# Attention layer with feed-forward on one core: causal weights cleared by GpSimd, normalisation transfers on SP, two head operations on ScalarE

## Chip, core and metric

The kernel runs on one core of one Trainium2 chip. The metric is the device time of one execution in microseconds (us), as a median over runs. Engines are named as in the profile: PE is TensorE, DVE is VectorE, ACT is ScalarE, POOL is GpSimd, SP is SyncE.

## The reference, cut to what matters

```python
# x: (4, 1024, 512), 16 heads of 32
mod = (silu(c) @ wmod).reshape(4, 6, 1, 512)          # sa, ca, ga, sb, cb, gb
h = layernorm(x) * (1 + ca) + sa
q = (layernorm(h, qn_g, qn_b) @ Wq + bq)              # k, v alike, with kvn and Wkv
q, k = rotary(q * scale, h), rotary(k * scale, h)     # turned, times the norm of h
qn, kn = layernorm(q, ln_g, ln_b), layernorm(k, ln_g, ln_b)   # over each head's 32
scores = where(causal, qn @ kn.T / sqrt(32), min)
a = softmax(scores) @ v
x = x + ga * (a @ Wo + bo)
h = layernorm(x) * (1 + cb) + sb
x = x + gb * ((silu(h @ Wg.T) * (h @ Wu.T)) @ Wd.T)
```

Everything is float32. Where precision needs it, products use the two halves (hi and lo) of a number in the type fp32r.

## The kernel before

Four stages run one after the other, each a block with one instruction stream per engine: `qkv_stage`, `attention_stage`, `project_stage`, `ffn_stage`. The streams meet at semaphores only; each engine takes its instructions strictly in the order in which they stand.

**qkv_stage** works through 32 tiles of 128 rows. `stagger` writes each engine's stream: step u runs the functions of a list in the order of the list, each on tile u minus its lag. In step u DVE runs `norm_h` (tile u-3), `norm_x` (u-1), `stat_h` (u-2), `stat_x` (u), `turn` (u-5, the rotary products out of PSUM), `low` (u-3), `means` (u-6), `spread` (u-7). ACT runs `scale_x` (u-1), `high` (u-3), `root_h`, `root_x`, `take_v` (u-5), `square_h` (u-2), `square_heads` (u-6), `factor` (u-7). POOL runs `shift_x` (u-1), `norm_heads` (u-8), `rotate` (u-5), `centre` (u-6). PE runs `turn_h` (u-3, four transposes) and `product` (u-4, 39 matmuls). The head normalisation of q and k goes through three engines: `rotate` on POOL, `means` on DVE (a sum over each head at L397 and its scaling to `hmean` at L399), `centre` on POOL, `square_heads` on ACT, `spread` on DVE (a sum at L404, `ms2h` at L405, `den` at L407, a reciprocal at L409), `factor` on ACT, `norm_heads` on POOL.

**attention_stage** works through 16 groups (a batch entry and four heads). A group has 12 steps k, numbered w = 0 to 11. In a step PE writes two shift matmuls of the step's block into `psB`, then two score items into `psA` (only their maximum over keys is taken, by DVE, `peak`), then two more shift matmuls, in w = 1 and 3 a transposition of q or k for the group ahead (`prepare`), in w = 0 the transposition of the peaks, and then `weigh` of the block shifted one step before: the weights `probT` times v into `psO` and times ones into `psL`. ACT turns each shift result into weights (`exponent`, L950), with two buffers in `psB` and three in `probT`. `BLOCKS` has 12 blocks a group, (half, kb); a block whose key tile touches the diagonal (8 of the 12, numbers 0 to 3 and 8 to 11) gets a mask matmul behind each of its four shift matmuls (L825). Blocks run 14 steps behind the scores: block 0 of a group in w = 2, block 11 in w = 1. The chain `prepare` (PE), `widen` (ACT), `high` (POOL, L753), `low` (DVE, L876) makes the next group's operands; score items and `prepare` take turns in the two halves of `psA`, so each waits for what stood two turns before.

`normalise(n)` on POOL sends the sums of the weights to DRAM, reads them back spread over 128 partitions, waits for DVE's reciprocal, writes them out, reads them back widened, and multiplies `att` with them (L767), all in w = 3 of group n+2:

```python
            def normalise(n):
                pool.wait_ge(s["taken_l"], 2 * n + 2)
                pool.dma_start(scratch["sums"][0], sums[0:P:HD, n % 2]).then_inc(s["sums_out"], 16)
                pool.wait_ge(s["sums_out"], 16 * n + 16)
...
                pool.wait_ge(s["wide_in"], 64 * n + 64)
                pool.wait_ge(s["taken_o"], 2 * n + 2)
                pool.tensor_tensor(att[:, n % 2], att[:, n % 2], sums[:, n % 2], ALU.mult).then_inc(s["scaled"], 1)
```

Of the kernel before, what the change touches and what calls it, by code (L numbers as in the profile page):

```python
# [111 lines left out]
def qkv_stage(nc, args, scratch):  # L112
# [4 lines left out]
    with ExitStack() as ctx:  # L117
# [3 lines left out]
        def sem(name):  # L121
# [28 lines left out]
        ms2h = sb("a_ms2h", [P, 8])  # L150
# [24 lines left out]
                 "rec_ready fac_ready qk_ready").split()  # L175
# [11 lines left out]
        rows1_out, mod_in = sem("rows1_out"), sem("mod_in")  # L187
        late_copied, late_step, late_out = sem("late_copied"), sem("late_step"), sem("late_out")
# [19 lines left out]
        def _(sp):  # L208
# [4 lines left out]
            def load(b, t):  # L213
# [36 lines left out]
            sp.wait_ge(late_step, 4)  # L250
            for m in range(2, 6):
                at, n = late_place(m)
                sp.wait_ge(late_copied, m - 1)
                sp.dma_start(scratch["mod"][:, m, :], late[at, n]).then_inc(late_out, 16)
            for j in range(4):
                sp.wait_ge(stored[j], 32 * NT // 4)
            sp.wait_ge(late_out, 16 * 4)
# [34 lines left out]
        def _(dve):  # L292
# [101 lines left out]
            def means(b, t):  # L394
# [15 lines left out]

            stagger(dve, B, TB, [(norm_h, 3), (norm_x, 1), (stat_h, 2), (stat_x, 0), (turn, 5), (low, 3), (means, 6), (spread, 7)])
# [4 lines left out]
            dve.tensor_scalar(size[two], late[two], -1.0, None, ALU.mult).then_inc(late_step, 1)  # L416
            dve.wait_ge(late_step, 1)
            dve.tensor_tensor(size[two], size[two], late[two], ALU.max).then_inc(late_step, 1)
            dve.wait_ge(late_step, 2)
            dve.tensor_scalar(size[two], size[two], 0.25, None, ALU.max).then_inc(late_step, 1)  # L420
            dve.wait_ge(late_step, 3)
            dve.scalar_tensor_tensor(out=late[two], in0=sign[two], scalar=-1.0, in1=size[two], op0=ALU.add, op1=ALU.mult).then_inc(late_step, 1)

        @block.scalar
        def _(act):
# [152 lines left out]
def attention_stage(nc, args, scratch):  # L578
# [12 lines left out]
    BUFS = 3  # L591

# [38 lines left out]
    with ExitStack() as ctx:  # L631
# [3 lines left out]
        def sem(name):  # L635
# [18 lines left out]
        probT = sb("b_probT", [P, 3, 4, W])  # L654
# [9 lines left out]
                 "peaks_turned peaks_copied peaks_in shifted expd weighed summed taken_o taken_l sums_out few_in inverted few_out "  # L664
# [17 lines left out]
        def _(sp):  # L682
# [36 lines left out]

            load(0)  # L720
# [4 lines left out]
            for k in STEPS:  # L725
# [9 lines left out]
                if w == 10 and 0 <= n - 2 < NG:  # L735
                    store(n - 2)
# [3 lines left out]
        def _(pool):  # L740
# [708 lines left out]
```

## Time and profile before

| | us |
|---|---|
| median of 3 runs | 2458.92 (2458.35 to 2460.32) |
| the profiled execution, its own time | 2456.73 |
| its span in the profile | 2454.6 |
| PE busy | 2279.7 (93%) |
| DVE busy | 1165.7 (47%) |
| ACT busy | 793.3 (32%) |
| POOL busy | 728.3 (30%) |

The busy shares are means over four stages that differ. qkv_stage ends near 392 us of the span, attention_stage runs from about 400 to about 1200, the feed-forward stage from about 1400 to the end. In the page's 40 slices DVE shows 9 tenths in the first stage and 5 in the second, and PE 9 in both.

### The profile page before, as it was taken

Reading aid. Unit: us, or ns where it says so; the run is one execution under the profiler, and the core shown is the slowest. Engines: PE = TensorE matmul, PEld = TensorE weight load, DVE = VectorE, ACT = ScalarE, POOL = GpSimd, SP = SyncE. Lnnn points to the kernel's source line nnn. Section 1 sums busy time; section 2 is a strip of 40 time slices with the busy share of each in tenths; the row PEclk is TensorE's granted clock in tenths of the full one; section 3 lists DMA queues with packets and bytes.
Section 4 is the critical chain, followed back from the end, with each engine's and each line's share of the span. In section 5 each row is a group of like instructions: output and inputs, shape, how many; then the busy total and the mean of one; then the engine's idle time right before and its main releaser. Section 6 shows DMA issues by size and latency. Waiting matters only on the chain. (4 is left out here: it accounts for less than half of the span.)

```text
span 2454.6 us, 32466 instructions
## 1 busy us (share of the span) xinstructions
PE 2279.7 (93%) x12520; PEld 1705.3 (69%) x12520; DVE 1165.7 (47%) x1799; ACT 793.3 (32%) x1671; POOL 728.3 (30%) x694
## 2 busy tenths in 40 slices
PE   6999992899999999999858799999999999999998
PEld 3777771666666666666446588888888888888887
DVE  5999994655555555555269611222222212121222
ACT  3333331255555555455435411111111111111111
POOL 2677674002112111111177122222222222222221
PEclk8999996699999999999989899999999999999999
DMA  6122224554465455443179511212121212111111
GB/s 223 69 103 90 98 98 120 122 128 117 102 149 126 106 135 139 111 102 89 37 244 308 204 48 52 69 48 69 52 69 49 68 53 68 44 58 49 48 56 52
DMA packets 161828, 243.70 MB, mean 99 GB/s; under 512 B 17124, under 2 KB 84292, under 8 KB 161184
## 3 DMA queue, kind: packets, MB, share of 16 engines
q1 hardware_dynamic: 153184, 220.66, 30.9%
q0 software_dynamic: 7456, 18.07, 2.5%
q10 hardware_dynamic: 1056, 3.15, 0.3%
q8 instruction: 91, 1.49, 0.2%
q14 instruction: 41, 0.34, 0.0%
HBM read 131.69 MB, written 59.26 MB: 78 GB/s over the span
## 5 line engine op out<-in xcount | busy, mean ns | idle before, releaser
L883 DVE TENSOR_REDUCE b_top<-b_psA 128x2 f32<-128x1024 f32 (+3 forms) x384 | 353.3, 954 | 246.0 <-PE b_psA L801 154.3
L950 ACT ACTIVATE b_probT<-b_psB 128x512 f32<-128x512 f32 (+3 forms) x768 | 338.7, 488 | 330.0 <-PE b_psB L825 242.3
L1313 DVE TENSOR_TENSOR f_gu<-f_psU,f_silu 128x512 f32<-128x512 f32 x128 | 88.5, 691 | 711.8 <-PE f_psU L1380 711.8
L1269 POOL TENSOR_SCALAR f_wd_hi<-f_wd 128x512 fp32r<-128x512 f32 x128 | 83.7, 654 | 822.5 <-PE f_psD L1365 775.6
L822 PE MATMUL b_psB<-b_stack 98*128 98x512 f32 (+3 forms) x768 | 268.2, 404 | 5.0 <-ACT b_probT L950 4.6
L801 PE MATMUL b_psA<-b_stack 96*128 96x512 f32 (+3 forms) x768 | 228.3, 387 | 30.2 <-DMA b_stack<-b_halves 20.3
L822 PEld LDWEIGHTS b_psB<-b_stack 98*128 98x128 f32 x768 | 140.6, 189 | 143.5 <-issue 99.8
L1289 ACT ACTIVATE f_silu<-f_psG 128x512 f32<-128x512 f32 x128 | 76.5, 598 | 503.8 <-PE f_psG L1380 503.8
L1378 PE MATMUL f_psG<-f_hT_hi,w_hi 128*128 128x512 f32 x512 | 200.2, 391 | 10.9 <-DVE f_hT_lo L1307 10.9
L1380 PE MATMUL f_psG<-f_hT_lo,w_hi 128*128 128x512 f32 x512 | 199.7, 390 | 0.0
L1379 PE MATMUL f_psG<-f_hT_hi,w_lo 128*128 128x512 f32 x512 | 199.7, 390 | 0.0
L1378 PE MATMUL f_psU<-f_hT_hi,w_hi 128*128 128x512 f32 x512 | 199.2, 389 | 0.0
L1380 PE MATMUL f_psU<-f_hT_lo,w_hi 128*128 128x512 f32 x512 | 199.2, 389 | 0.0
L1379 PE MATMUL f_psU<-f_hT_hi,w_lo 128*128 128x512 f32 x512 | 199.2, 389 | 0.0
L1364 PE MATMUL f_psD<-f_wd_lo,f_gu_hi 128*128 128x512 f32 x512 | 199.2, 389 | 0.0
L1363 PE MATMUL f_psD<-f_wd_hi,f_gu_hi 128*128 128x512 f32 x512 | 199.2, 389 | 0.0
L1365 PE MATMUL f_psD<-f_wd_hi,f_gu_lo 128*128 128x512 f32 x512 | 199.2, 389 | 0.0
L1284 ACT ACTIVATE f_gu_hi<-f_gu 128x512 fp32r<-128x512 f32 x128 | 80.9, 632 | 364.5 <-DVE f_gu L1313 364.5
L801 PEld LDWEIGHTS b_psA<-b_stack 96*128 96x128 f32 x768 | 145.2, 200 | 51.6 <-issue 21.7
L1271 POOL TENSOR_TENSOR f_wd_lo<-f_wd,f_wd_hi 128x512 fp32r<-128x512 f32 x128 | 168.5, 1316 | 10.6
L840 PE MATMUL b_psO<-b_probT,b_v 128*32 128x512 f32 (+3 forms) x1536 | 163.6, 498 | 0.0
L840 PE MATMUL b_psL<-b_probT,b_ones 128*32 128x512 f32 (+3 forms) x1536 | 159.0, 486 | 0.0
(177 smaller groups left out, 4136.2 us busy)
## 6 DMA issues: line engine op xcount, KB each, us to landing
b_stack<-b_halves SPq DMA_DIRECT2D x192, 256.0 KB, 5.1
f_wd<-in_wd_t SPq DMA_DIRECT2D x128, 256.0 KB, 2.6
qkv_d<-a_t SPq DMA_DIRECT2D x32, 512.0 KB, 2.7
b_land<-qkv_d SPq DMA_DIRECT2D x32, 512.0 KB, 4.6
a_x<-in_x SPq DMA_DIRECT2D x32, 256.0 KB, 3.2
qkv_d<-a_v SPq DMA_DIRECT2D x32, 256.0 KB, 3.0
b_v<-qkv_d SPq DMA_DIRECT2D x16, 512.0 KB, 5.9
att_d<-b_att SPq DMA_DIRECT2D x16, 512.0 KB, 3.2
```

The costliest lines, as they stand in the source:

```text
L801: mm = pe.matmul(out[:, h, 0:hi - lo], stack[0:ROWS, n % BUFS, 1, j, t * P:(t + 1) * P], stack[0:ROWS, n % BUFS, 0, j, lo:hi], start=True, ...
L822: mm = pe.matmul(psB[:, i % 2, cols], stack[0:NR, n % BUFS, 0, j, kb * P:(kb + 1) * P], stack[0:NR, n % BUFS, 1, j, first * P:(half + 1) * ...
L840: mm = pe.matmul(out[rows, (first - half * HALF) * P:W], ones[:] if summing else v[:, n % 2, kb, rows], probT[:, (NW * n + w) % 3, j, 0:(h ...
L883: dve.tensor_reduce(out, slot("score", NI * n + i)[:, :, 0:width], AX.X, ALU.max, negate=True).then_inc(s["maxed"], 1)
L950: act.activation(probT[:, (NW * n + w) % 3, j, 0:width], psB[:, i % 2, 0:width], ACT.Exp).then_inc(s["expd"], 1)
L1271: pool.tensor_tensor(wd_lo[:, u % 2], wd[:, u % 2], wd_hi[:, u % 2].bitcast(F32), ALU.subtract).then_inc(s["wd_lo"], 1)
L1363: pe.matmul(out_t, gu_hi[:, u % 2, cols], wd_hi[:, u % 2], start=first, stop=False)
L1364: pe.matmul(out_t, gu_hi[:, u % 2, cols], wd_lo[:, u % 2], start=False, stop=False)
L1365: mm = pe.matmul(out_t, gu_lo[:, u % 2, cols], wd_hi[:, u % 2], start=False, stop=end)
L1378: pe.matmul(out_c, w_hi[:, m, k, cols], hi, start=(k == 0), stop=False)
L1379: pe.matmul(out_c, w_lo[:, m, k, cols], hi, start=False, stop=False)
L1380: mm = pe.matmul(out_c, w_hi[:, m, k, cols], lo, start=False, stop=(k == KC - 1))
```

## The change

It has four parts.

- In qkv_stage `hmean` is made on ACT (`mean_heads`, ahead of `square_heads`), `den` too (`denominator`, first in ACT's list); `ms2h` is gone, its factor sits in the square. `spread` keeps the sum alone and stands ahead of `turn` in DVE's list; the reciprocal is a function of its own, `invert`, at the end of the list.
- In attention_stage the mask matmul behind the shift matmuls is gone. POOL clears the upper triangle of `probT` after the exponentials (`cut`, one affine_select of 128x4x128 for each diagonal block), and `weigh` of these blocks waits for it. The masks of the score items stay.
- The transfers of `normalise` are issued by SP: out in w = 9 and back in w = 10 of group n+2, the reciprocal on DVE in w = 0, out in w = 1, widened in w = 2, the multiplication on POOL in w = 3 of group n+3, in two halves, and the store in w = 5.
- Some semaphores are merged, and `PROBS = 3` names the number of `probT` buffers, as before.

```diff
             def means(b, t):
...
                 dve.tensor_reduce(hsum[:, t % 4], r, AX.X, ALU.add).then_inc(s["sums"], 1)
-                dve.wait_ge(s["sums"], done(b, t))
-                dve.tensor_scalar(hmean[:, t % 4], hsum[:, t % 4], -1.0 / HD, None, ALU.mult).then_inc(s["means"], 1)
...
-                dve.tensor_reduce(vsum[:, t % 4], t1[:, t % 4].rearrange("p (h d) -> p h d", d=HD), AX.X, ALU.add)
-                dve.tensor_scalar(ms2h[:, t:t + 1], ms2[:, t:t + 1], 1.0 / HD, None, ALU.mult).then_inc(s["rec_ready"], 1)
-                dve.wait_ge(s["rec_ready"], thrice(b, t, 1))
-                dve.tensor_scalar(den[:, t % 4], vsum[:, t % 4], ms2h[:, t:t + 1], EPS, ALU.mult, ALU.add).then_inc(s["rec_ready"], 1)
-                dve.wait_ge(s["rec_ready"], thrice(b, t, 2))
+                dve.tensor_reduce(vsum[:, t % 4], t1[:, t % 4].rearrange("p (h d) -> p h d", d=HD), AX.X, ALU.add).then_inc(s["vsums"], 1)
+
+            def invert(b, t):
+                dve.wait_ge(s["dens"], done(b, t))
                 dve.reciprocal(rec[:, t % 4], den[:, t % 4]).then_inc(s["rec_ready"], 1)
 
-            stagger(dve, B, TB, [(norm_h, 3), (norm_x, 1), (stat_h, 2), (stat_x, 0), (turn, 5), (low, 3), (means, 6), (spread, 7)])
+            stagger(dve, B, TB, [(norm_h, 3), (norm_x, 1), (stat_h, 2), (stat_x, 0), (spread, 7), (turn, 5), (low, 3), (means, 6), (invert, 7)])
...
+            def mean_heads(b, t):
+                act.wait_ge(s["sums"], done(b, t))
+                act.activation(hmean[:, t % 4], hsum[:, t % 4], ACT.Copy, scale=-1.0 / HD).then_inc(s["means"], 1)
+
+            def denominator(b, t):
+                act.wait_ge(s["vsums"], done(b, t))
+                act.activation(den[:, t % 4], vsum[:, t % 4], ACT.Identity, scale=ms2[:, t:t + 1], bias=eps[:, 0:1]).then_inc(s["dens"], 1)
...
-            stagger(act, B, TB, [(scale_x, 1), (high, 3), (root_h, 2), (root_x, 0), (take_v, 5), (square_h, 2), (square_heads, 6), (factor, 7)])
+            stagger(act, B, TB, [(denominator, 7), (scale_x, 1), (high, 3), (root_h, 2), (root_x, 0), (take_v, 5), (square_h, 2), (mean_heads, 6), (square_heads, 6), (factor, 7)])
...
+            def cut(n, w):
+                pool.wait_ge(s["expd"], 4 * (NW * n + w) + 4)
+                square = probT[:, (NW * n + w) % PROBS, :, 0:P]
+                pool.affine_select(out=square, in_=square, compare_op=ALU.is_ge, fill=0.0, base=0,
+                                   pattern=[[0, 4], [1, P]], channel_multiplier=-1).then_inc(s["cut"], 1)
...
             for k in STEPS:
+                if cut_at(k):
+                    cut(*cut_at(k))
                 if prep_at(k):
                     high(*prep_at(k))
-                at = take_at(k)
-                if at and at[1] == 1 and at[0] < NG - 1:
-                    normalise(at[0])
+                n, w = unit(k)
+                if w == 3 and 0 <= n - 3 < NG - 1:
+                    normalise(n - 3)
...
-                if first == kb:
-                    mm = pe.matmul(psB[:, i % 2, 0:P], mask_r[:], ident_r[:], start=False, stop=True, skip_group_check=True)
                 mm.then_inc(s["shifted"], 1)
...
                 if not summing:
-                    pe.wait_ge(s["expd"], 4 * (NW * n + w) + 4)
+                    if w in DIAGONAL:
+                        pe.wait_ge(s["cut"], len(DIAGONAL) * n + DIAGONAL.index(w) + 1)
+                    else:
+                        pe.wait_ge(s["expd"], 4 * (NW * n + w) + 4)
```

ACT in qkv_stage, a steady step, before (`a_fac` is `factor`, `a_h<-a_h,a_rs` is `scale_x`):

```order
L493 ACTIVATE a_t<-a_t 128x1024
L496 ISA
L497 ACTIVATE a_fac<-a_rec,a_ms 128x32
L469 ACTIVATE a_h<-a_h,a_rs 128x512
L47 REGISTER_ALU
L484 ACTIVATE hT_hi<-a_psT 128x512
L479 ACTIVATE a_sd<-a_mv,a_eps 128x1
L455 REGISTER_ALU
L456 ACTIVATE a_sd<-a_mv,a_eps 128x1
L47 REGISTER_ALU
L489 ACTIVATE a_v<-a_psQ 128x512
L474 ACTIVATE a_junk,a_ms<-a_h 128x512
```

and with the change (`a_den` is `denominator`, `a_hmean` is `mean_heads`):

```order
L497 ACTIVATE a_fac<-a_rec,a_ms 128x32
L493 ACTIVATE a_den<-a_vsum,a_eps,a_ms 128x32
L461 ACTIVATE a_h<-a_h,a_rs 128x512
L47 REGISTER_ALU
L476 ACTIVATE hT_hi<-a_psT 128x512
L471 ACTIVATE a_sd<-a_mv,a_eps 128x1
L447 REGISTER_ALU
L448 ACTIVATE a_sd<-a_mv,a_eps 128x1
L47 REGISTER_ALU
L481 ACTIVATE a_v<-a_psQ 128x512
L466 ACTIVATE a_junk,a_ms<-a_h 128x512
L489 ACTIVATE a_hmean<-a_hsum 128x32
```

`denominator` stands between `factor` and `scale_x`, so `scale_x` of a step now follows `spread` of the same step.

DVE in qkv_stage, a steady step, before, from `low` to `norm_h` (`a_hn`):

```order
L375 TENSOR_TENSOR hT_lo<-a_psT,hT_hi 128x512
L395 REGISTER_ALU
L397 TENSOR_REDUCE a_hsum<-a_t 128x32
L399 TENSOR_SCALAR a_hmean<-a_hsum 128x32
L404 TENSOR_REDUCE a_vsum<-a_t 128x32
L405 TENSOR_SCALAR a_ms2h<-a_ms 128x1
L406 ISA
L407 TENSOR_SCALAR a_den<-a_vsum,a_ms2h 128x32
L408 REGISTER_ALU
L409 RECIPROCAL a_rec<-a_den 128x32
L364 RECIPROCAL a_rs<-a_sd 128x1
L367 TENSOR_SCALAR a_hn<-a_h,a_mv,a_rs 128x512
```

and with the change, from the end of `stat_x` to `norm_h` (`a_vsum` is `spread`, `a_t<-a_psQ,cos_t` begins `turn`, `a_hsum` is `means`, `a_rec` is `invert`):

```order
L327 BN_AGGR a_mv<-a_stats 128x2
L397 TENSOR_REDUCE a_vsum<-a_t 128x32
L47 REGISTER_ALU
L382 TENSOR_TENSOR a_t<-a_psQ,cos_t 128x1024
L385 TENSOR_TENSOR a_t<-a_psQ,sin_t 128x512 x2
L370 TENSOR_TENSOR hT_lo<-a_psT,hT_hi 128x512
L390 REGISTER_ALU
L392 TENSOR_REDUCE a_hsum<-a_t 128x32
L401 RECIPROCAL a_rec<-a_den 128x32
L359 RECIPROCAL a_rs<-a_sd 128x1
L362 TENSOR_SCALAR a_hn<-a_h,a_mv,a_rs 128x512
L331 RECIPROCAL a_rs<-a_sd 128x1
```

The three operations between the sums and the reciprocal are gone from DVE, and the sum of `spread` has moved from the end of the step to the place ahead of `turn`.

POOL in attention_stage, one group, before (`b_halves` is `high`, `b_att` the multiplication of `normalise`):

```order
L753 TENSOR_SCALAR b_halves<-b_whole 128x1024 x2
L757 DMA sums_d<-b_sums 4x1024
L759 DMA b_few<-sums_d 128x32
L761 DMA sums_d<-b_few 128x32
L764 DMA b_sums<-sums_d 32x1024 x4
L767 TENSOR_TENSOR b_att<-b_att,b_sums 128x1024
```

and with the change:

```order
L792 AFFINE_SELECT b_probT<-b_probT 128x4x128 x2
L787 TENSOR_SCALAR b_halves<-b_whole 128x1024
L800 TENSOR_TENSOR b_att<-b_att,b_sums 128x512 x2
L792 AFFINE_SELECT b_probT<-b_probT 128x4x128 x6
L787 TENSOR_SCALAR b_halves<-b_whole 128x1024
```

The two halves of the multiplication follow the second `high` of a group with nothing between, where the first transfer stood; the cuts fill the other places.

## Rows read from the trace of the kernel before

**Rows 1.** Busy time of each engine in stretches of 50 us (PE, PEld, DVE, ACT, POOL).

```profile
200.00:250.00 50.00, 45.32 (x201) 35.40 (x200) 47.53 (x93) 17.66 (x40) 35.92 (x23) 1.00 0.30 105
700.00:750.00 50.00, 49.53 (x390) 31.76 (x383) 27.21 (x33) 25.56 (x55) 10.17 (x11) 1.00 0.48 118
1250.00:1300.00 50.00, 39.62 (x176) 30.22 (x175) 45.93 (x81) 23.20 (x67) 39.52 (x46) 0.99 0.81 268
```

**Rows 2.** Groups by line in qkv_stage: busy us, mean ns, idle before.

```profile
L404 DVE TENSOR_REDUCE a_vsum<-a_t 128x32 f32<-128x1024 f32 x32 | 38.6, 1206 | 0.7 <-ACT a_t L493 0.7
...
L399 DVE TENSOR_SCALAR a_hmean<-a_hsum 128x32 f32<-128x32 f32 x32 | 29.0, 905 | 1.1
L407 DVE TENSOR_SCALAR a_den<-a_vsum,a_ms2h 128x32 f32<-128x32 f32 x32 | 26.1, 815 | 1.1
...
L497 ACT ACTIVATE a_fac<-a_rec,a_ms 128x32 f32<-128x32 f32 x32 | 9.8, 305 | 2.4 <-DVE a_rec L409 2.4
```

**Rows 3.** Timeline of a steady step of qkv_stage: start us, us, engine, line.

```profile
206.26 0.55 DVE L367 TENSOR_SCALAR a_hn<-a_h,a_mv,a_rs 128x512 f32<-128x512 f32 x1
...
207.80 0.72 ACT L469 ACTIVATE a_h<-a_h,a_rs 128x512 f32<-128x512 f32 x1 [0.79 <-DVE a_h L346]
...
208.75 1.29 POOL L273 TENSOR_TENSOR a_h<-a_h,mod 128x512 f32<-128x512 f32 x1
...
209.34 1.20 DVE L387 TENSOR_TENSOR a_t<-a_psQ,cos_t 128x1024 f32<-128x1024 f32 x1
...
210.00 1.91 POOL L287 TENSOR_TENSOR a_t<-a_t,a_fac 128x1024 f32<-128x1024 f32 x1
...
211.88 2.39 POOL L277 TENSOR_TENSOR a_t<-a_t 128x1024 f32<-128x1024 f32 x1
...
214.39 1.91 POOL L281 TENSOR_TENSOR a_t<-a_t,a_hmean 128x1024 f32<-128x1024 f32 x1
...
216.33 1.06 ACT L493 ACTIVATE a_t<-a_t 128x1024 f32<-128x1024 f32 x1 [5.49 <-POOL a_t L281]
...
216.86 0.55 DVE L367 TENSOR_SCALAR a_hn<-a_h,a_mv,a_rs 128x512 f32<-128x512 f32 x1
```

**Rows 4.** Timelines: DVE beside POOL, early in qkv_stage and in ffn_stage.

```profile
53.70 2.40 POOL L277 TENSOR_TENSOR a_t<-a_t 128x1024 f32<-128x1024 f32 x1 [6.93 <-DVE a_t L390]
...
54.32 2.06 DVE L367 TENSOR_SCALAR a_hn<-a_h,a_mv,a_rs 128x512 f32<-128x512 f32 x1
...
1402.41 1.59 POOL L1271 TENSOR_TENSOR f_wd_lo<-f_wd,f_wd_hi 128x512 fp32r<-128x512 f32 x1
...
1402.79 1.77 DVE L1307 TENSOR_TENSOR f_hT_lo<-f_land,f_hT_hi 128x512 fp32r<-128x512 f32 x1
...
1403.98 1.05 POOL L1269 TENSOR_SCALAR f_wd_hi<-f_wd 128x512 fp32r<-128x512 f32 x1
```

**Rows 5.** Timeline of attention_stage, PE: a step without mask matmuls, a step with them.

```profile
735.47 0.73 PE L822 MATMUL b_psB<-b_stack 98*128 98x512 f32 x2
736.05 0.69 PE L801 MATMUL b_psA<-b_stack 96*128 96x512 f32 x3
...
743.39 0.50 PE L822 MATMUL b_psB<-b_stack 98*128 98x512 f32 x1
...
744.13 0.85 PE L801 MATMUL b_psA<-b_stack 96*128 96x512 f32 x3
```

**Rows 6.** Timeline of attention_stage, around the second prepare of a group.

```profile
718.79 0.86 PEld L786 LDWEIGHTS b_psA<-b_ident,b_land 128*128 128x128 f32 x8 [0.55 <-DVE b_top L883]
...
721.27 1.05 POOL L753 TENSOR_SCALAR b_halves<-b_whole 128x1024 fp32r<-128x1024 f32 x1 [6.99 <-ACT b_whole L939]
...
722.35 1.23 DVE L876 TENSOR_TENSOR b_halves<-b_whole,b_halves 128x1024 fp32r<-128x1024 f32 x1 [3.01 <-POOL b_halves L753]
...
723.49 2.08 DVE L883 TENSOR_REDUCE b_top<-b_psA 128x2 f32<-128x1024 f32 x2
...
725.70 0.90 PE L801 MATMUL b_psA<-b_stack 96*128 96x512 f32 x3
```

More of the change, by code:

```diff
@@ L253, in _ @@
                 sp.wait_ge(late_copied, m - 1)
-                sp.dma_start(scratch["mod"][:, m, :], late[at, n]).then_inc(late_out, 16)
+                sp.dma_start(scratch["mod"][:, m, :], late[at, n]).then_inc(rows_out, 16)
             for j in range(4):
                 sp.wait_ge(stored[j], 32 * NT // 4)
-            sp.wait_ge(late_out, 16 * 4)
+            sp.wait_ge(rows_out, 16 * 6)
         @block.gpsimd
@@ L415, in _ @@
             dve.tensor_scalar(sign[two], late[two], 0.0, 2.0, ALU.is_ge, ALU.mult)
[L416 to L422, printed above, removed]
+            dve.tensor_scalar(size[two], late[two], -1.0, None, ALU.mult).then_inc(small_dve, 1)
+            dve.wait_ge(small_dve, DVE_ROW + 1)
+            dve.tensor_tensor(size[two], size[two], late[two], ALU.max).then_inc(small_dve, 1)
+            dve.wait_ge(small_dve, DVE_ROW + 2)
+            dve.tensor_scalar(size[two], size[two], 0.25, None, ALU.max).then_inc(small_dve, 1)
+            dve.wait_ge(small_dve, DVE_ROW + 3)
+            dve.scalar_tensor_tensor(out=late[two], in0=sign[two], scalar=-1.0, in1=size[two], op0=ALU.add, op1=ALU.mult).then_inc(small_dve, 1)
         @block.scalar
@@ L591, in attention_stage @@
     BUFS = 3
+    PROBS = 3
     def unit(k):
@@ L613, in weigh_at, with cut_at @@
         return shift_at(k - 1)
+    DIAGONAL = [w for w, (half, kb) in enumerate(BLOCKS) if kb >= half * HALF]
+    def cut_at(k):
+        at = shift_at(k)
+        return at if at and at[1] in DIAGONAL else None
     def take_at(k):
@@ L718, in store, with sums_out, few_in, few_out @@
                 sp.dma_start(dst, att[:, n % 2].rearrange("p (t q) -> p t q", q=P)).then_inc(stored, 16)
+            def sums_out(n):
+                sp.wait_ge(s["taken_l"], 2 * n + 2)
+                sp.dma_start(scratch["sums"][0], sums[0:P:HD, n % 2]).then_inc(s["sums_out"], 16)
+            def few_in(n):
+                sp.wait_ge(s["sums_out"], 16 * n + 16)
+                sp.dma_start(few[:, 0], scratch["sums"][0].rearrange("j (a c) -> (j a) c", c=C // HD)).then_inc(s["few_in"], 16)
+            def few_out(n):
+                sp.wait_ge(s["inverted"], n + 1)
+                sp.dma_start(scratch["sums"][1].rearrange("j (a c) -> (j a) c", c=C // HD), few[:, 1]).then_inc(s["few_out"], 16)
+            def wide_in(n):
+                sp.wait_ge(s["few_out"], 16 * n + 16)
+                for j in range(4):
+                    sp.dma_start(sums[j * HD:(j + 1) * HD, n % 2], scratch["sums"][1, j:j + 1].broadcast_to([HD, C])).then_inc(s["wide_in"], 16)
             load(0)
@@ L734, in _ @@
                     load_v(n)
-                if w == 10 and 0 <= n - 2 < NG:
-                    store(n - 2)
+                if 0 <= n - 2 < NG - 1:
+                    if w == 9:
+                        sums_out(n - 2)
+                    if w == 10:
+                        few_in(n - 2)
+                if 0 <= n - 3 < NG - 1:
+                    if w == 1:
+                        few_out(n - 3)
+                    if w == 2:
+                        wide_in(n - 3)
+                if w == 5 and 0 <= n - 3 < NG:
+                    store(n - 3)
             sp.wait_ge(stored, 16 * NG)
@@ L840, in weigh @@
                     mm = pe.matmul(out[rows, (first - half * HALF) * P:W], ones[:] if summing else v[:, n % 2, kb, rows],
-                                   probT[:, (NW * n + w) % 3, j, 0:(half + 1) * W - first * P],
+                                   probT[:, (NW * n + w) % PROBS, j, 0:(half + 1) * W - first * P],
                                    start=(kb == 0), stop=(kb == (half + 1) * HALF - 1), skip_group_check=True)
@@ L922, in _ @@
                     low(*prep_at(k))
-                at = take_at(k - 5)
-                if at and at[1] == 1 and at[0] < NG - 1:
-                    dve.wait_ge(s["few_in"], 16 * at[0] + 16)
+                n, w = unit(k)
+                if w == 0 and 0 <= n - 3 < NG - 1:
+                    dve.wait_ge(s["few_in"], 16 * (n - 3) + 16)
                     dve.reciprocal(few[:, 1], few[:, 0]).then_inc(s["inverted"], 1)
```

41 lines of the change are left out of this document (16 added, 25 removed).

## Prediction

> **What bounds the kernel now.** I read the page first, then stretches of 50 us, because the busy shares are means over four stages. In the first stage DVE is busy 47.5 of 50 us and PE 45.3; in attention PE is busy 49.5 and DVE 27 [rows 1]. So operations taken off DVE can pay in qkv_stage, and matmuls taken off PE in attention. The change does both, and it also puts an order of its own on the engines. That order is what I follow below, because neither stage has only one limit.
>
> The groups by line show what is odd in qkv_stage: `hmean` takes 905 ns and `den` 815 ns on 128x32 numbers, while `factor`, of the same size, takes 305 ns on ACT [rows 2]. The timelines tell why. At 54.32 DVE starts the `norm_h` scaling, which takes 0.55 us in the steady step [rows 3], and is held for 2.06 us: it ends at 56.38, which is 0.28 us after POOL's `rotate` ends at 56.10 [rows 4]. A DVE operation of this kind waits while POOL reads SBUF. Operations with two SBUF inputs wait too: the subtraction at 1402.79 takes 1.77 us and ends 0.56 us after POOL's does at 1404.00. At such a handover the waiting engine goes first: POOL's next operation, started at 1403.98, ends only at 1405.03, 0.47 us after DVE's 1404.56 [rows 4]. The tensor_reduce of `spread` and the products out of PSUM aren't held: 1206 ns in the mean [rows 2], 1.20 us at 209.34 beside a POOL operation [rows 3].
>
> **The change in qkv_stage.** It takes `hmean` and `den`, 1.72 us, and a third small operation off DVE for each tile, 55 us over 32 tiles if nothing else ended the wait. A step now takes 10.60 us (206.26 to 216.86 [rows 3]).
>
> What takes their place: `denominator` is first in ACT's list and waits for `spread` of the same step, so `scale_x` stands behind it; POOL's list starts with `shift_x`, which waits for `scale_x`; `centre`, last in POOL's list, feeds `square_heads` on ACT, and that feeds the next step's `spread`. This is a ring through one step with no slack. From the end of `spread`: a hop and `den` at the price of `factor`, 0.1 + 0.3 [rows 2]; from the start of `scale_x` to `shift_x` 0.95; to `norm_heads` 1.25; to `rotate` 1.88; `rotate` 2.39; `centre` 1.91; `square_heads` 0.03 + 1.06 [rows 3]; a hop of 0.05 and `spread` 1.21 [rows 2]. The sum is 11.1 us, already above 10.60.
>
> Then the port. Call the end of `spread` T, where `turn` starts. Before, `norm_h` scaled at 7.52 us after `turn` started (209.34 to 216.86 [rows 3]); without `hmean`, the sum of `spread`, `den` and `ms2h`, that is 2.9 us less, so T + 4.6. POOL, whose work starts at T + 1.3 by the ring, begins `rotate` at T + 4.4 and ends it at T + 6.8. So `norm_h` is held to T + 7.1 and `centre` runs from T + 7.1 to T + 9.0. `norm_x` (two SBUF inputs) arrives at T + 7.3, is held until then and ends at T + 9.5. Two statistics follow (some 1.6 us, from the start of `scale_x`, which follows `norm_x`, to `turn` [rows 3]), then `spread`: T + 12.2. `square_heads` is done at T + 10.1 and no longer decides. PE needs about 9.7 us a step (45.3 of 50 us busy [rows 1], of 10.6) and stays ahead; its clock should hold, since at 39.6 of 50 us busy it was granted 0.99 [rows 1]. Steps with the whole ring run from u = 8 to 32, 25 of them: 25 x (12.2 - 10.6) = **+40 us**. The last steps have no `shift_x`, and there the two operations leave a pure chain: -2. The stage gets +38. Bounds: the ring without any hold gives 25 x 0.5 - 2 = +10; if POOL went first at each handover, a step would take 12.7 and the stage +50. If `norm_h` arrives 0.2 us sooner, ahead of `rotate`, it is served at once and only `norm_x` is held: 11.8 and +28. I take 12.2, since each hold has its row.
>
> The Trainium skill (SBUF — State Buffer, "SBUF: two separate sides") speaks against the change here: the port pair of DVE and GpSimd is an exclusive lock, and whoever starts second blocks for the whole instruction. By that rule alone, without the ring, the stage would be judged by how long the two overlap; the rows on `norm_h` agree with it.
>
> **The change in attention_stage.** 512 mask matmuls go (8 blocks x 4 x 16). With masks, from the first shift matmul to the scores takes 0.74 us (743.39 to 744.13), without 0.58 (735.47 to 736.05) [rows 5]: 0.08 us for each mask. No row has a narrow block without its mask; the mean pace of all PE instructions, 50 us over 390 or 0.13 [rows 1], is the other end. I take 0.09, near the measured one.
>
> Not all count. Between the two `prepare` of a group PE is tied to `widen`, `high`, `low` and DVE's maxima: at 718.79 it already waits 0.55 us for DVE [rows 6]. The 8 masks of blocks 0 and 1 only lengthen that wait. After the second `prepare`, `high` ends at 722.32 and `low` starts at 722.35; DVE's maxima end at 725.57, and PE's second score item behind 725.70 needs them [rows 6]: the 6 masks up to there bring little. 18 masks a group are left, 18 x 0.09 x 15 groups = 24 us, and 2 for the last group, which has no scores beside it.
>
> Here the moved multiplication costs. It used to wait for its transfers; now its inputs are long there, and both halves stand right behind the second `high`, where `low` (two SBUF inputs) starts. POOL starts a next operation 0.03 us before its last one ends (211.88 against 210.00 + 1.91 [rows 3]) and so leads DVE by 0.06. The first half holds `low` for 1.1 us (1.28 for 512 columns, like `shift_x` [rows 3]), then DVE goes first. PE's score item comes 1.1 us later than now and had some 0.6 us in hand: +0.5 x 12 groups = +6. If DVE wins the race, it is -7 instead; if both halves hold it, +20.
>
> The cuts: 128, each between the end of a block's exponentials and its `weigh`, about 3 us later. At the price of POOL's 1.29 us for 512 columns [rows 3], none is late; `high`, with one input, takes 1.05 for twice the columns [rows 6], so a cut may take half as long. Block 2 is nearest: it waits for both halves and has some 1.5 us. The transfers on SP stand behind the copy of the peaks in its queue and wait where SP had waited anyway; nobody needs their result for most of a group: 0.
>
> Attention gets -24 - 2 + 6 = **-20 us**, between -3 and -45.
>
> **Sum.** +38 - 20 = +18. On the profiled execution that is 2456.7 + 18 = 2474.7; the median of the runs is 2.2 higher, so I say 2477. A measurement can tell about 0.2%, 5 us, from no change.
>
> **Rivals.**
> - *Forecast: ring and port* (0.56). 2477, from about 2456 (+28 in the first stage, DVE wins the race) to 2492. It is slower beyond 0.2% in 0.49, within it in 0.05, faster in 0.02.
> - *Ring without holds* (0.22): DVE and POOL drift so that `norm_h` and `norm_x` miss POOL's operations. +10 - 20 = -10, so 2449, or 2434 if attention has no race either. Against it: both stand in fixed places behind `spread`. Faster 0.18, same 0.04.
> - *DVE is simply relieved* (0.12), faster where I say slower: `spread` comes early enough that the step falls to PE's 9.7. It decides if POOL's list is done 1.4 us earlier than by the ring. 25 x -0.9 - 20 = -43, so 2416. For it stands that DVE is the busiest there [rows 1]; against it, the ring. The Trainium skill (VectorE: DVE Perf Modes, "Rules for kernel authors") says to reduce the number of DVE operations; three fewer a tile would by that rule be this case.
> - *The cut is late* (0.10), slower: if a cut takes over 1.6 us, `weigh` of block 2 and then others wait. At twice 1.29 us that is 1 us in 15 to 30 places: 2492 to 2507.
>
> **How the numbers follow.** Slower 0.49 + 0.10, rounded to 0.59; same 0.05 + 0.04 = 0.09; faster 0.02 + 0.18 + 0.12 = 0.32. The range 2432 to 2492 takes in the first two cases with their bounds and leaves out the relieved DVE and most of the late cuts, some 2 in 10.
>
> **What would show it.** Right: a step of 12.2 us in qkv_stage, DVE and PE both idle there; `norm_h` near 2.7 us and `norm_x` near 2.2 instead of 0.55 and 0.75; ACT's `den` waiting for DVE; a group of attention some 1.3 us shorter; `low` held once a group. Wrong: a step at 11.1 with `norm_h` at 0.55 (second case), a step below 10 with PE without waits (third), PE waiting for POOL ahead of the weights (fourth).

## The result, and the profile after

The changed kernel takes 2665.02 us (median of 4 runs, 2663.55 to 2666.39) against 2459.1 us for the kernel before (4 runs): a ratio of 1.0837, 95% interval 1.0818 to 1.0856. It is 206 us slower where +18 was forecast, far outside the range. The profiled execution took 2663.55 us, its span 2661.8.

Where the time came from is read off the first thing that POOL does in a stage, the memset of the identity. The changed kernel:

```profile
445.11 0.20 POOL L106 MEMSET b_ident<- 128x128 f32 x1 [7.88 <-POOLq L117]
...
1436.89 0.21 POOL L106 MEMSET p_ident<- 128x128 f32 x1 [6.76 <-POOLq L638]
```

In the kernel before these stand at 399.97 and 1228.85. So qkv_stage has become 45.1 us longer (445.11 - 399.97), attention_stage 162.9 us (991.78 against 828.88), and the rest, 1224.9 against 1225.8 us, has not changed. The two stages have different causes.

**attention_stage.** The page's stretches of 50 us (columns as in [rows 1]) for both stages of the changed kernel:

```profile
200.00:250.00 50.00, 40.91 (x165) 32.29 (x166) 48.55 (x69) 17.88 (x44) 30.23 (x21) 0.90 0.24 84
750.00:800.00 50.00, 36.09 (x269) 20.46 (x261) 18.45 (x24) 19.21 (x42) 4.49 (x7) 0.86 0.37 89
```

PE's 49.53 us of 50 in attention [rows 1] have become 36.09, and DVE's 27.21 have become 18.45: both wait. The waits of 560 to 1380 us say for what (engine, line and tile that waited, what ended it: us in total, times, longest):

```profile
DVE b_att L936 <- DMA att_d<-b_att: 183.0, 12, 15.9
PE b_psO L877 <- DVE b_att L936: 157.5, 12, 13.8
```

Twelve times DVE's copy of `psO` into `att` waits 15 us for the **store** of `att`, and PE waits for the copy. One of the twelve in the timeline:

```profile
867.61 3.50 POOL L800 TENSOR_TENSOR b_att<-b_att,b_sums 128x512 f32<-128x512 f32 x2
870.06 13.62 SPq L710 DMA_DIRECT2D b_stack<-b_halves  x12
883.73 1.23 SPq L703 DMA_DIRECT2D b_v<-qkv_d  x1
885.00 1.34 SPq L725 DMA_DIRECT2D att_d<-b_att  x1
892.31 0.69 DVE L936 COPY b_att<-b_psO 128x512 f32<-128x512 f32 x1 [15.88 <-DMA att_d<-b_att]
893.15 1.94 PE L877 MATMUL b_psO<-b_probT,b_v 128*32 128x512 f32 x8 [13.76 <-DVE b_att L936]
```

SP's queue issues the twelve transfers of `lay_stacks` (w = 4) one after another for 13.6 us, then `load_v`, and only then the store (w = 5), whose data had been ready since POOL's multiplication ended at 871.11 (867.61 + 3.50). `att` has two buffers, so `take` of the group two later, in w = 7, which writes the same buffer, needs that store. Before, the burst of the stacks took as long, but the store stood 21 us ahead of it (the kernel before, two rows of SP's queue):

```profile
702.83 0.39 SPq L718 DMA_DIRECT2D att_d<-b_att  x1
...
723.65 14.07 SPq L703 DMA_DIRECT2D b_stack<-b_halves  x12
```

In the changed kernel, from one group to the next, by the start of POOL's `high` (L787, before L753), it takes 61.44 us:

```profile
805.16 1.05 POOL L787 TENSOR_SCALAR b_halves<-b_whole 128x1024 fp32r<-128x1024 f32 x1 [1.56 <-ACT b_whole L976]
...
866.60 1.05 POOL L787 TENSOR_SCALAR b_halves<-b_whole 128x1024 fp32r<-128x1024 f32 x1 [1.56 <-ACT b_whole L976]
```

and 47.26 before (721.27 [rows 6], the next at 768.53). 12 groups x 14.2 us are 170; the groups without the wait are shorter than before (two of them take 45.2 us by the same measure), which brings it to 163.

**qkv_stage.** DVE's groups by line, 100 to 350 us, with one of ACT (busy us, mean ns of one, idle before):

```profile
L362 DVE TENSOR_SCALAR a_hn<-a_h,a_mv,a_rs 128x512 f32<-128x512 f32 x21 | 82.7, 3940 | 2.9 <-DVE a_rs L359 0.9
...
L392 DVE TENSOR_REDUCE a_hsum<-a_t 128x32 f32<-128x1024 f32 x20 | 24.1, 1207 | 0.0
L397 DVE TENSOR_REDUCE a_vsum<-a_t 128x32 f32<-128x1024 f32 x20 | 23.7, 1186 | 0.0
L341 DVE SCALAR_TENSOR_TENSOR a_h<-a_x,a_mv,mod 128x512 f32<-128x512 f32 x20 | 23.0, 1149 | 3.2 <-DVE a_rs L331 1.0
```
```profile
L493 ACT ACTIVATE a_den<-a_vsum,a_eps,a_ms 128x32 f32<-128x32 f32 x20 | 8.3, 414 | 50.3 <-DVE a_vsum L397 50.3
```

`norm_h`, 0.55 us of work [rows 3], takes 3.94 us in the mean. ACT waits 50.3 us in 20 steps for `spread` ahead of `den`: the ring is there. The step is the distance of two `spread` (L397). DVE beside POOL in the timeline:

```profile
186.60 2.40 POOL L272 TENSOR_TENSOR a_t<-a_t 128x1024 f32<-128x1024 f32 x1
186.64 2.65 DVE L362 TENSOR_SCALAR a_hn<-a_h,a_mv,a_rs 128x512 f32<-128x512 f32 x1
188.97 2.09 POOL L276 TENSOR_TENSOR a_t<-a_t,a_hmean 128x1024 f32<-128x1024 f32 x1
189.62 1.99 DVE L341 SCALAR_TENSOR_TENSOR a_h<-a_x,a_mv,mod 128x512 f32<-128x512 f32 x1 [0.26 <-DVE a_rs L331]
193.16 1.19 DVE L397 TENSOR_REDUCE a_vsum<-a_t 128x32 f32<-128x1024 f32 x1
...
205.25 1.19 DVE L397 TENSOR_REDUCE a_vsum<-a_t 128x32 f32<-128x1024 f32 x1
...
217.84 1.19 DVE L397 TENSOR_REDUCE a_vsum<-a_t 128x32 f32<-128x1024 f32 x1
...
223.44 2.39 POOL L272 TENSOR_TENSOR a_t<-a_t 128x1024 f32<-128x1024 f32 x1
223.47 4.53 DVE L362 TENSOR_SCALAR a_hn<-a_h,a_mv,a_rs 128x512 f32<-128x512 f32 x1
225.80 1.90 POOL L276 TENSOR_TENSOR a_t<-a_t,a_hmean 128x1024 f32<-128x1024 f32 x1
...
230.52 1.19 DVE L397 TENSOR_REDUCE a_vsum<-a_t 128x32 f32<-128x1024 f32 x1
```

There are two kinds of step. Of the 23 from 80.77 to 368.07 us, 7 take 12.1 to 12.2 us and 16 take 12.6 to 12.8. At 186.64 `norm_h` is held through `rotate`, goes ahead of `centre`, and `centre` then holds `norm_x`: the step around it and the next take 12.1 (193.16 to 205.25). At 223.47 it is held through `rotate` and `centre` and ends 0.30 us after both: 12.6 to 12.7 (217.84 to 230.52). The mean from 168.21 to 230.52 is 12.46 us over 5 steps, against 10.60 before.

### The profile page after: what moved, and what is told of

The parts are those of the page before. It is cut to its first block and busy times, and to the rows that moved or that the text cites. A ratio compares the mean times of both kernels' runs of the same rounds, so it can differ in the third digit from the quotient of the medians.

```text
span 2661.8 us, 31485 instructions
## 1 busy us (share of the span) xinstructions
PE 2280.7 (86%) x12008; PEld 1663.9 (63%) x12008; DVE 1212.3 (46%) x1703; ACT 803.8 (30%) x1735; POOL 768.2 (29%) x732
## 5 line engine op out<-in xcount | busy, mean ns | idle before, releaser
L877 PE MATMUL b_psO<-b_probT,b_v 128*32 128x512 f32 (+3 forms) x1536 | 174.8, 528 | 157.6 <-DVE b_att L936 157.5
L792 POOL TENSOR_SCALAR_AFFINE_SELECT b_probT<-b_probT 128x512 f32<-128x512 f32 x128 | 81.2, 635 | 707.8 <-ACT b_probT L987 707.8
L858 PE MATMUL b_psB<-b_stack 98*128 98x512 f32 (+3 forms) x768 | 245.6, 397 | 6.6 <-ACT b_probT L987 6.6
L858 PEld LDWEIGHTS b_psB<-b_stack 98*128 98x128 f32 x768 | 125.3, 191 | 158.0 <-issue 106.1
```

The lines of the kernel that those rows point to most:

```text
L858: mm = pe.matmul(psB[:, i % 2, cols], stack[0:NR, n % BUFS, 0, j, kb * P:(kb + 1) * P], stack[0:NR, n % BUFS, 1, j, first * P:(half + 1) * ...
L877: mm = pe.matmul(out[rows, (first - half * HALF) * P:W], ones[:] if summing else v[:, n % 2, kb, rows], probT[:, (NW * n + w) % PROBS, j, ...
```

## Experiments

The diffs are cut to the lines that matter. All times are medians; the kernel before ran beside each batch and took 2457.85 (e1 to e4), 2458.45 (e5 to e8), 2457.3 (e9, e10) and 2459.55 us (e11, e12).

**e1, the change in qkv_stage alone.** Everything else is that of before.

```diff
-            stagger(dve, B, TB, [(norm_h, 3), (norm_x, 1), (stat_h, 2), (stat_x, 0), (turn, 5), (low, 3), (means, 6), (spread, 7)])
+            stagger(dve, B, TB, [(norm_h, 3), (norm_x, 1), (stat_h, 2), (stat_x, 0), (spread, 7), (turn, 5), (low, 3), (means, 6), (invert, 7)])
```

> The kernel before with the qkv_stage of the change alone. Theory (the ring through ACT and POOL, and the SBUF port that holds DVE's norm_h): the first stage is 45 us longer, as in the changed kernel, and nothing else moves, so 2504 us. Rival (part of these 45 us comes from the merged semaphores or from the attention part): under 2490 us.

Measured: 2504.13, ratio 1.0185 (1.0168 to 1.0202), +46 us, as the stage's own +45.1.

**e2, the transfers on SP alone.** To the kernel before: SP's four functions, the multiplication in w = 3 and the store in w = 5. The mask matmuls stay and nothing is cut.

```diff
-                if w == 10 and 0 <= n - 2 < NG:
-                    store(n - 2)
...
+                if w == 5 and 0 <= n - 3 < NG:
+                    store(n - 3)
```

> The kernel before with the transfers, multiplication and store of the change in attention_stage, but with the mask matmuls and without the cuts. Theory (the store of att stands behind the twelve transfers of the stacks in SP's queue, take on DVE waits for it, and psO holds up PE): PE still waits 11 to 14 us in 12 of the groups, 2459 + 150 to 190, so 2610 to 2650 us. Rival (the cuts on POOL hold up the weights, the transfers are harmless): 2459 us within 5.

Measured: 2647.17, ratio 1.0774 (1.0756 to 1.0792). The move of the transfers, with the two held halves of the multiplication in it (e4 and e7), makes +189 us by itself; POOL's cuts have no share in it.

**e3, the changed kernel with the store ahead of the stacks.**

```diff
+                if w == 4 and 0 <= n - 3 < NG:
+                    store(n - 3)
                 if w == 4 and n + 1 < NG:
                     lay_stacks(n + 1)
...
-                if w == 5 and 0 <= n - 3 < NG:
-                    store(n - 3)
```

> The changed kernel with the store of att ahead of the transfers of the stacks in SP's queue (w = 4, before lay_stacks). Theory of the store: the waits of DVE and PE on it vanish and attention_stage falls below its 829 us of before, to about 800 to 815, so the kernel takes 2475 to 2492 us (the first stage keeps its +45). Rival (the cuts, or the multiplication in w = 3 itself): it stays above 2600 us.

Measured: 2490.85, ratio 1.014 (1.0123 to 1.0157). One call moved by one step gives 174 us back. attention_stage takes 816.9 us, 12.0 less than before and 2 more than the expected 800 to 815. Its timeline, the store now ahead of the stacks and the copy without a wait for it:

```profile
857.13 3.50 POOL L800 TENSOR_TENSOR b_att<-b_att,b_sums 128x512 f32<-128x512 f32 x2
860.66 0.38 SPq L725 DMA_DIRECT2D att_d<-b_att  x1
861.15 9.36 SPq L710 DMA_DIRECT2D b_stack<-b_halves  x8
867.76 0.69 DVE L936 COPY b_att<-b_psO 128x512 f32<-128x512 f32 x1 [0.21 <-PE b_psO L877]
```

**e4, the same attention_stage with qkv_stage of before.** The diff is that of e3, on the changed attention_stage alone.

> The kernel before with the attention_stage of the change and the store ahead of the stacks: e3 without the part in qkv_stage. If the parts add, it is e3 less 45 us: 2430 to 2447 us, faster than the kernel before by the mask matmuls. If qkv_stage's change moved something else, the difference from e3 is not 45.

Measured: 2450.15 (8 runs, 2441.15 to 2454.02), ratio 0.9962 (0.9948 to 0.9976). The parts add roughly: e3 less e4 is 41 us where e1 gave 46. In the profiles qkv_stage differs by 45.5 us, and attention_stage, the same code in both, by 3.9 the other way (816.9 in e3, 820.8 in e4). The gain of 8 us is short of the expected 11 to 28. The groups and the clock show what is missing. Here are POOL's multiplication in the groups by line, one collision, and PE in stretches of 4 us behind it (busy us, granted clock):

```profile
L800 POOL TENSOR_TENSOR b_att<-b_att,b_sums 128x512 f32<-128x512 f32 x28 | 47.0, 1697 | 0.0
```
```profile
716.05 3.49 POOL L800 TENSOR_TENSOR b_att<-b_att,b_sums 128x512 f32<-128x512 f32 x2
716.12 2.30 DVE L913 TENSOR_TENSOR b_halves<-b_whole,b_halves 128x1024 fp32r<-128x1024 f32 x1 [3.02 <-POOL b_halves L787]
...
719.61 1.37 PE L837 MATMUL b_psA<-b_stack 96*128 96x512 f32 x3 [0.60 <-DVE b_top L920]
```
```profile
716.00:720.00 4.00, 3.40 (x28) 1.00 0.66 199
720.00:724.00 4.00, 3.87 (x26) 0.74 0.92 227
724.00:728.00 4.00, 4.00 (x28) 0.50 0.98 203
...
732.00:736.00 4.00, 4.00 (x18) 0.55 1.02 215
736.00:740.00 4.00, 4.00 (x28) 1.00 0.75 195
```

The first half holds `low` by 1.07 us (2.30 against 1.23 [rows 6]), `low` goes next and holds the second half, and PE waits for DVE. A group takes 46.23 us, and this one 52.33: after some waits of up to 0.6 us the granted clock goes from 1.00 to 0.50 (1.2 GHz) for about 14 us. These waits alone don't decide it: one group earlier, from 662 to 674 us, PE has the same wait of 0.60 us and is busy 3.33, 3.67 and 3.40 us of each 4, and the clock stays at 1.00. Before, each stretch of 50 us from 550 to 1200 had 1.00.

**e5, the ring cut.** qkv_stage of the change, attention_stage of before; the diffs of e5, e6 and e8 are against e1.

```diff
-            stagger(act, B, TB, [(denominator, 7), (scale_x, 1), (high, 3), ...
+            stagger(act, B, TB, [(scale_x, 1), (denominator, 7), (high, 3), ...
```

> The attention of before with the change's qkv_stage, in which denominator stands behind scale_x on ACT (e1 has it first). Ring theory (a step of the changed qkv_stage is the chain spread, denominator, scale_x, shift_x, norm_heads, rotate, centre, square_heads, and POOL's two holds of norm_h and norm_x are added to it): scale_x and shift_x no longer wait for spread, the ring is cut, and the step falls from 12.5 to about 10.3 us although norm_h and norm_x can be held as before; 25 steps give 2445 to 2458. Rival (the step is long because DVE's own list with its held TENSOR_SCALARs fills it, whatever ACT's order is): at least 12 us a step, 2490 to 2504, as e1. Expected: 2450.

Measured: 2445.99, ratio 0.9949 (0.9933 to 0.9966): 58 us below e1. The step is 10.2 us (`spread` at 150.92 and 161.10), with `norm_x` still held:

```profile
L341 DVE SCALAR_TENSOR_TENSOR a_h<-a_x,a_mv,mod 128x512 f32<-128x512 f32 x22 | 44.7, 2033 | 3.4 <-DVE a_rs L331 1.0
...
L362 DVE TENSOR_SCALAR a_hn<-a_h,a_mv,a_rs 128x512 f32<-128x512 f32 x24 | 17.4, 725 | 3.3 <-DVE a_rs L359 0.9
```

**e6, `norm_h` out of POOL's way, the ring kept.**

```diff
-            stagger(dve, B, TB, [(norm_h, 3), (norm_x, 1), (stat_h, 2), (stat_x, 0), (spread, 7), (turn, 5), ...
+            stagger(dve, B, TB, [(norm_x, 1), (stat_h, 2), (stat_x, 0), (spread, 7), (norm_h, 3), (turn, 5), ...
```

> The attention of before with the change's qkv_stage, ACT's order of the change kept (denominator first), and norm_h moved behind spread in DVE's list, away from the stretch in which POOL does rotate and centre. Theory (ring of 11.1 us, the rest of the 12.5 us is the held norm_h): only the holds go, the mean of norm_h falls from 3.9 us to under 2.5 us, and the step is about 11.3 us: 2470 to 2484. Rival (the holds are hidden beside the ring): no gain, 2500 or more. Expected: 2476.

Measured: 2493.1, ratio 1.0144 (1.0127 to 1.0161), a miss of both expectations. The hold had not gone, it had changed its victim:

```profile
L341 DVE SCALAR_TENSOR_TENSOR a_h<-a_x,a_mv,mod 128x512 f32<-128x512 f32 x22 | 76.9, 3496 | 3.5 <-DVE a_rs L331 1.0
...
L362 DVE TENSOR_SCALAR a_hn<-a_h,a_mv,a_rs 128x512 f32<-128x512 f32 x21 | 11.5, 547 | 2.3
```

`norm_h` is free (547 ns), and `norm_x`, now the first operation to come up against `rotate` and `centre`, takes 3.50 us in the mean. Again there are two kinds of step: 12.0 where `norm_x` takes 4.0 us (200.64 to 212.63), and 11.5 where it takes some 2.1 (189.17 to 200.64). So the ring of 11.1 us alone wasn't seen in this run.

**e7, e4 with the multiplication a step earlier.** The diff is against e4.

```diff
-                if w == 3 and 0 <= n - 3 < NG - 1:
+                if w == 2 and 0 <= n - 3 < NG - 1:
                     normalise(n - 3)
```

> e4 (attention of the change with the stores issued ahead of the next group's stacks, qkv_stage of before) with the multiplication normalise, that gives the two halves to POOL, taken in step w=2 of a group instead of w=3. Theory (in e4 POOL's two multiplications fall on DVE's low, which is held by about 1 us, and PE waits for it in 12 groups): that wait of PE goes, and with it some of the stretches in which the granted clock of e4 falls (0.79 at 725 to 750 us, 0.84 at 450 to 550): 2430 to 2444. Rival (the clock falls because PE has less to do in each group without the mask matmuls, wherever POOL works): 2446 to 2452, no change against e4. Expected: 2441.

Measured: 2431.58, ratio 0.9892 (0.9875 to 0.9908), 19 us below e4. The multiplication is free of holds:

```profile
L800 POOL TENSOR_TENSOR b_att<-b_att,b_sums 128x512 f32<-128x512 f32 x28 | 35.2, 1279 | 0.7 <-DMA b_sums<-sums_d 0.7
```

A group now takes 45.15 us where the clock stays at 1.00. The rival expected no change and is out; but five of the twelve stretches of 50 us from 550 to 1150 still show a clock of 0.97, and five groups take 46.56 to 46.67, 1.5 us more than the others.

**e8, the same operations in the order of before.** qkv_stage of the change, attention_stage of before.

```diff
-            stagger(dve, B, TB, [(norm_h, 3), ..., (stat_x, 0), (spread, 7), (turn, 5), (low, 3), (means, 6), (invert, 7)])
-            stagger(act, B, TB, [(denominator, 7), (scale_x, 1), ..., (mean_heads, 6), (square_heads, 6), (factor, 7)])
+            stagger(dve, B, TB, [(norm_h, 3), ..., (stat_x, 0), (turn, 5), (low, 3), (means, 6), (spread, 7), (invert, 7)])
+            stagger(act, B, TB, [(scale_x, 1), ..., (mean_heads, 6), (denominator, 7), (square_heads, 6), (factor, 7)])
```

> The attention of before with the change's qkv_stage of parts (root_h, root_x, square_h, mean_heads and denominator where the change has them, on the same engines) but DVE's order of before (spread and invert last) and ACT in the order scale_x, high, root_h, root_x, take_v, square_h, mean_heads, denominator, square_heads, factor. Theory (the move of work off DVE is worth something once neither the ring nor a hold sets the step): the step is under 10.5 us of before, about 9.7, and the time 2434 to 2448. Rival (POOL's four operations or a hold on DVE set the step at 10.5 us as before): 2455 to 2460. Expected: 2440.

Measured: 2431.58, ratio 0.9893 (0.9877 to 0.991), 2.4 us under the expected range and 73 us below e1 with the same operations on the same engines. A step takes 9.6 us, and PE sets it (first row a stretch, then two groups):

```profile
200.00:250.00 50.00, 50.00 (x227) 40.36 (x226) 45.22 (x87) 23.89 (x57) 39.34 (x27) 1.00 0.33 116
```
```profile
L362 DVE TENSOR_SCALAR a_hn<-a_h,a_mv,a_rs 128x512 f32<-128x512 f32 x24 | 20.9, 873 | 3.3 <-DVE a_rs L359 0.9
...
L341 DVE SCALAR_TENSOR_TENSOR a_h<-a_x,a_mv,mod 128x512 f32<-128x512 f32 x22 | 16.5, 752 | 3.4 <-DVE a_rs L331 1.0
```

**e9, qkv_stage of e8 and attention_stage of e7.** The diffs of both.

> The qkv_stage of e8 and the attention_stage of e7 together. Theory (the two stages don't touch each other, so the parts add, as e1, e2, e3 and e4 did): 2431.6 + 2431.6 - 2458.5 = 2404.7; range 2400 to 2411. Rival (with PE less busy in both stages the granted clock falls more often, or the qkv_stage that ends earlier finds the attention's first loads no earlier): 2412 to 2425. Expected: 2405.

Measured: 2403.55 (2402.54 to 2405.86), ratio 0.9785 (0.9772 to 0.9798). It is the fastest of all: 2.15% under the kernel before and 261 us under the changed one, with the whole of the change in it.

**e10, e7 with the mask matmuls kept.** The diff is against e7.

```diff
+                if first == kb:
+                    mm = pe.matmul(psB[:, i % 2, 0:P], mask_r[:], ident_r[:], start=False, stop=True, skip_group_check=True)
                 mm.then_inc(s["shifted"], 1)
...
-                if cut_at(k):
-                    cut(*cut_at(k))
```

> e7 with the second kind of mask matmuls kept (those of L825 of before) and GpSimd's cuts gone: what the exchange of the 512 mask matmuls is worth by itself, once the store and the multiplication stand well. Prediction's term (18 matmuls a group of 0.09 us, 15 groups and 2 us at the end): 2431.6 + 26 = 2458, and PE busy 99% as before. Clock theory (without the masks PE is busy some 97.5% and its granted clock falls to 0.97 in about every second stretch of 50 us, with them it stays at 1.00, so part of the gain was given back): 2446 to 2454. Rival (POOL's cuts cost PE's chain as much as they save): 2432 to 2440. Expected: 2452.

Measured: 2457.67, ratio 1.0001 (0.9992 to 1.001). The exchange of matmuls for cuts is worth 26 us; what is left of the attention change, the transfers on SP, then costs and gains nothing. PE's stretch at 700 us is that of before again:

```profile
700.00:750.00 50.00, 49.55 (x391) 30.99 (x388) 27.22 (x33) 25.91 (x57) 4.63 (x4) 1.00 0.48 118
```

I had expected 2452, a lower value, since I took the clock's losses off my own term. A group takes 47.23 us here and 45.15 in e7 at full clock, which would be 2.08 x 15 = 31 us. The dips take some of it back: five groups of e7 at 1.5 us more make about 7. The rest of the difference to 26 lies in the first and last groups, which don't have this pace. Here every stretch of 50 us from 500 to 1200 has a clock of 1.00, so the dips came with the exchange of the matmuls for the cuts.

**e11, the changed kernel with three buffers for `att`.** Nothing is moved.

```diff
-        att = sb("b_att", [P, 2, C])
+        att = sb("b_att", [P, 3, C])
...
-                at_least(dve, stored, 16 * (n - 1))
+                at_least(dve, stored, 16 * (n - 2))
```

> The changed kernel, nothing moved, but with three buffers for att in place of two: take(n) then waits for the multiplication and the store of group n-3, not n-2. The store stays behind the twelve transfers of lay_stacks in SP's queue. Theory (the 163 us in attention_stage are the wait of the two-buffered att for a store that comes 12 us late; the late store itself hurts nobody): the wait goes, as in e3, and the time is 2480 to 2496. Rival (it is the traffic of the store beside the stacks, or SP's queue, that delays the group): 2600 or more. Expected: 2489.

Measured: 2497.4, ratio 1.0157 (1.014 to 1.0174). The store is as late as in the changed kernel, and no one waits:

```profile
876.46 1.24 SPq L725 DMA_DIRECT2D att_d<-b_att  x1
...
899.55 0.68 DVE L936 COPY b_att<-b_psO 128x512 f32<-128x512 f32 x1
```

So it is the two-buffered `att` that turned a late store into a stall, not traffic. The time is 1 us above my bound of 2496, and its profile has two groups of 52.3 us, the clock dip of e4, where that of e3 has none so long (four of 47.8).

**e12, the changed kernel with three calls moved** (the diffs of e3, e5 and e7).

> The changed kernel with three calls moved: denominator behind scale_x (e5), the store ahead of lay_stacks (e3), the multiplication in w=2 (e7). Theory (the parts add): 2458 - 12.5 - 26.9 = 2419; range 2414 to 2426. Rival (the parts disturb one another): outside of it. Expected: 2419.

Measured: 2419.75, ratio 0.9834 (0.9818 to 0.985). By the stages, e5 and e7, the parts add to within 1 us (2419). Counted down from the changed kernel, 174 + 58 + 19 = 251 us would give 2414, 6 below the measured time.

## Why the prediction was wrong

The side was right and the size was not. Without the late store (e3) the time would have been 2490.85, 14 us above the 2477 of the forecast and just inside the range: 7 of them in qkv_stage (+45 for +38) and 8 in attention_stage (-12 for -20). By the steps of the prediction:

- **The step that failed is the one on SP's transfers: "The transfers on SP [...] nobody needs their result for most of a group: 0".** I followed the four transfers of the sums and not the fifth, the store, which the change had moved behind the multiplication and therefore behind the stacks in SP's queue. What waits for it is `take` of the group two later, which writes the same buffer, and it comes not "most of a group" but two steps after the store, in w = 7. In place of 0 stands +174 us (the changed kernel against e3), and e11 shows the same by the buffer (168 us).
- **The ring and the port, +38 us.** The mechanism held, and the size within its bounds of +10 and +50: +45.1 us. The step was forecast at 12.2, or 12.7 if POOL goes first at each handover; both occur, 12.1 and 12.6 to 12.8, and the mean is 12.46. The miss is that I took DVE as winning each handover, from one pair of rows in ffn_stage [rows 4]. e5 shows that the ring is what makes the stage long: without it the holds of `norm_x` remain and the step is 10.2. The hold of `norm_h` went with the ring, though (0.73 us in the mean), so the shares of the two are not separated. The 11.1 us of the ring alone were never seen by themselves, since e6 moved the hold. PE's clock, which I said should hold, did not: the stretches from 100 to 400 us have 0.90 to 0.97 (0.90 at 200 to 250, with PE busy 40.91). PE waits in this stage in any case, so the steps of 12.1 and 12.6 came out as forecast.
- **The masks, -26 us.** e10 against e7 gives 26, the sum forecast. This is partly luck: a group at full clock gets 2.08 us shorter where the sum has 18 x 0.09 = 1.62, and the clock takes about 7 us back, a term that I didn't have.
- **The multiplication against `low`, +6 us.** The collision is as forecast, in the order forecast: first half, `low`, second half. The size was wrong: e4 to e7 is 19 us, near my bound of +20 for both halves. I had subtracted 0.6 us of slack; a group of e4 takes 46.23 against 45.15 in e7, so all of the 1.07 us hold reaches PE, some 13 us over 12 groups. In the profiled executions the whole stage gets 16.8 us shorter (820.8 to 804.0). The clock dips explain little of the rest: one group of 52.3 us and two of 47.8 make about 9 us in e4, and the five of e7 about 7. What is left, to 19, stays open; the runs of e4 lie between 2441 and 2454.
- **The cuts, nothing.** Nearly right: from 560 to 1380 us 26 waits of `weigh` for a cut make 4.3 us in all, none over 0.2. A cut of 128x512 takes 635 ns, the lower of the two prices I gave.
- **The sum of what was measured.** 45 + 174 - 26 + 19 = 212 us, 6 over the measured 206. As e3 less e4 and e12 show too, the parts add to within 5 or 6 us, no closer; the same attention_stage took 816.9 us in e3's profile and 820.8 in e4's.
- **Rivals.** That DVE is simply relieved got 0.12 and lost in the order of the change, but e8 shows that it was the order and not the operations: PE's 9.6 us are reached (9.7 in that rival). The low end of the forecast's own case, 2456, should read about 2454 by its terms (28 - 26 - 7 = -5), which changes nothing. The Trainium skill (VectorE: DVE Perf Modes, "Rules for kernel authors"), which says to reduce the number of DVE operations, comes out both ways with one set of operations: +46 us in e1 and -27 in e8.

The Trainium skill (SBUF — State Buffer, "SBUF: two separate sides") says of the pair that whichever starts first has it "for the whole instruction". The trace agrees for `norm_h` at 186.64, which ends 0.29 us after `rotate`; at 223.47 `norm_h` is held through two instructions of POOL, 4.53 us for 0.55 us of work, which goes beyond what the page states.

## What to carry to other kernels

When a change moves one transfer, list what stands ahead of **every** transfer of that chain in its new queue, with issue times, and name for each the next writer of its buffer; here the one that cost 174 us was the last of the chain. When operations go to another engine, keep their place in each in-order list late enough that nothing of the same step stands behind a wait on the other engine: one entry's place was worth 58 us here and the whole order 73, the operations themselves 27. Moving one victim of a hold at the SBUF port out of the way can hand POOL's operations the next one: e6 freed `norm_h` and gained 11 of the 46 us, while the order of e8 left both nearly free (873 and 752 ns).

## What was not expected of the hardware

- At a handover of the SBUF port either engine may go first. Starts of `norm_h` within 0.04 us of `rotate`'s start led to 2.65 us (held once, 186.64) and to 4.53 us (held through both, 223.47). What decides it stays open. In e4 DVE's `low`, with two SBUF inputs, went ahead of POOL's second half.
- What is held depends on the operation: beside the same POOL operations TENSOR_REDUCE keeps its 1186 to 1207 ns, and TENSOR_SCALAR and SCALAR_TENSOR_TENSOR of 0.55 and 0.75 us go up to 3.94 and 3.50 in the mean.
- The granted clock fell to 0.50 with PE busy 3.4 to 3.5 us of each 4 before it and a last wait of 0.60 us for DVE (e4, 708 to 720 us), and stayed there while PE was busy all the time, 724 to 732; one group earlier it stayed at 1.00 with the same wait and much the same busy time, so what tips it stays open. In the changed kernel it is 0.50 from 884 to 892 us, in 12 us without a matmul. The Trainium skill (TensorE: Matmul & The Clock Gate, "A second HAM failure mode: psum-queue depth-cycling") tells of re-throttling by frequent short idles between groups of matmuls. e4 agrees in kind for this group, and its neighbour with the same idles kept 1.00. Taking matmuls off a PE that was 99% busy cost some of the gain here, about 7 us (e7 against e10).
